# A linear-attention step on one core: the state product regrouped by pairs of sequences, and VectorE's step reordered

## The reference

```python
xn  = layernorm(x)
q   = softmax(exp(beta) * (xn @ Wq.T + bq), over the 8 features of a head)
k   = softmax(exp(beta) * (xn @ Wk.T + bk), over the 8 features of a head)
v   = xn @ Wv.T + bv
kv  = cumsum over tokens of k^T v        # per head an 8x8 state
kn  = cumsum over tokens of k
att = (q @ kv) / sum(q * kn)
ffn = fp8_round(xn) @ weight_fp8.T + bias
out = x + att @ Wo.T + bo + ffn
```

## Time and profile before

| | before |
|---|---|
| time, median of 3 runs | 1250.92 us (1249.5 to 1252.77) |
| span of the profiled execution, first to last instruction | 1248.2 us |
| PE busy | 1174.9 us, 94% of the span |
| DVE busy | 977.9 us, 78% |
| ACT busy | 744.9 us, 60% |
| POOL busy | 321.6 us, 26% |
| chain that ended last | PE 92%, issue 3%, DVE 2%, DMA, ACT and POOL 1% each |
| granted PE clock, mean over the span | 0.982 of full speed |

### The profile page before, as it was taken

One profiled execution on the slowest core, in us unless ns is written; L12 is line 12 of the kernel. 1 busy time (PEld: TensorE's weight loads), 2 busy tenths in 40 slices (PEclk: granted clock), 3 DMA queues, 4 the chain that ended last, 5 costly groups with the idle time before them and its releaser, 6 DMA issues.

```text
span 1248.2 us, 60447 instructions
## 1 busy us (share of the span) xinstructions
PE 1174.9 (94%) x26082; PEld 679.2 (54%) x26082; DVE 977.9 (78%) x1968; ACT 744.9 (60%) x1177; POOL 321.6 (26%) x590
## 2 busy tenths in 40 slices
PE   1459999999999999999999999999999999999996
PEld 1235555555555555555555555555555555555553
DVE  4567887888788788878878887788788778878873
ACT  0456656665666666566666656666665666566652
POOL 3122222322222232222223232222323232222310
PEclk9689999999999999999999999999999999999999
DMA  9022334334334433433333343343343433333331
GB/s 234 21 59 70 81 90 89 78 80 91 82 82 87 89 80 79 90 86 80 85 89 82 77 90 89 78 84 91 81 79 91 84 83 81 91 82 81 72 73 46
DMA packets 156483, 104.64 MB, mean 84 GB/s; under 512 B 111968, under 2 KB 128480, under 8 KB 156256
## 3 DMA queue, kind: packets, MB, share of 16 engines
q1 hardware_dynamic: 155536, 99.76, 35.7%
q10 hardware_dynamic: 720, 1.31, 0.4%
HBM read 40.20 MB, written 16.78 MB: 46 GB/s over the span
## 4 chain that ended last, share of the span: by engine, by line
PE 92%; issue 3%; DVE 2%; DMA 1%; ACT 1%; POOL 1%; SPq 0%; POOLq 0%; DVEq 0%; ACTq 0%
PE s_ps L900 10%; PE a_ps L917 7%; PE a_ps L1018 6%; PE a_ps L999 6%; PE k_ps L873 5%; PE vo_ps L975 5%; PE vo_ps L873 5%; PE k_ps L877 5%; PE k_ps L875 5%; PE vo_ps L884 4%; PE vo_ps L888 4%; PE vo_ps L886 4%; PE vo_ps L877 4%; PE vo_ps L875 4%; PE q_ps L877 4%; PE q_ps L873 4%
## 5 line engine op out<-in xcount | busy, mean ns | idle before, releaser
L521 ACT ACTIVATE q_heads<-qT,cst 128x512 f32<-128x512 f32 x256 | 163.9, 711 | 88.2 <-DVE qT L769 88.2
L407 POOL TENSOR_TENSOR y_sum<-y,y_magic 128x512 f32<-128x512 f32 x64 | 81.4, 1272 | 433.0 <-DVE y_magic L629 433.0
L506 ACT ACTIVATE w_own<-kT,cst 128x512 f32<-128x512 f32 x128 | 85.5, 715 | 166.7 <-DVE kT L711 166.7
L530 ACT ACTIVATE st_seqs<-st_run,cst 128x576 f32<-128x576 f32 x252 | 181.5, 797 | 0.5 <-DVE st_run L665 0.5
L671 DVE TENSOR_TENSOR att<-s_ps,cst 128x512 f32<-128x512 f32 x256 | 163.8, 682 | 0.4 <-PE s_ps L900 0.4
L400 POOL TENSOR_TENSOR x_split<-xn,x_split 128x512 f16<-128x512 f32 x64 | 74.1, 1158 | 291.6 <-ACT x_split L462 284.3
L900 PE MATMUL s_ps<-q_heads,w_own 64*64 64x128 f32 x4096 | 141.3, 275 | 0.6 <-DVE att L671 0.6
L900 PEld LDWEIGHTS s_ps<-q_heads,w_own 64*64 64x64 f32 x4096 | 110.4, 132 | 54.3 <-issue 54.2
L462 ACT ACTIVATE x_split<-xn 128x512 f16<-128x512 f32 x64 | 40.3, 630 | 126.7 <-DVE xn L618 126.7
L873 PE MATMUL k_ps<-w_hi,xT 128*128 128x512 f16 x256 | 98.9, 386 | 17.0 <-DMA xT<-x_split 12.3
L727 DVE TENSOR_TENSOR vp<-vo_ps,vp 128x512 f32<-128x512 f32 x64 | 44.3, 692 | 86.3 <-PE vo_ps L877 86.3
(11 more groups left out here) (136 smaller groups left out, 2287.8 us busy)
## 6 DMA issues: line engine op xcount, KB each, us to landing
v_groups<-vp SPq DMA_DIRECT2D x512, 36.0 KB, 3.1
x_in<-L_attn_x SPq DMA_DIRECT2D x64, 256.0 KB
x_res<-L_attn_x SPq DMA_DIRECT2D x64, 256.0 KB
out<-o_sb SPq DMA_DIRECT2D x64, 256.0 KB
w_own<-L_attn_Wk SPq DMA_DIRECT2D x1, 1024.0 KB, 13.0
w_own<-L_attn_Wq SPq DMA_DIRECT2D x1, 1024.0 KB, 15.0
w_own<-L_attn_Wv SPq DMA_DIRECT2D x1, 1024.0 KB, 16.5
att<-L_ffn_weight_fp SPq DMA_DIRECT2D x1, 1024.0 KB, 18.1
```

The lines of the kernel that those rows point to most:

```text
L506: last = sc.activation(k_pairs[:, i.parity, :, c, :], kT[:, :, :], ACT.Copy, scale=pair_mask[:, c:c + 1])
L521: last = sc.activation(q_heads[:, i.parity, :, j, :], qT[:, i.parity, :, :], ACT.Copy, scale=head_mask[:, j:j + 1])
L530: last = sc.activation(st_seqs[:, i.parity, :, :, b, :].rearrange("p g j w -> p (g j) w"), st_run[:, :, :, :].rearrange("p g j w -> p (g j ...
```

## The change

Four things change, all inside a round.

1. **State product.** It becomes 32 matmuls instead of 64: for each of 16 head groups and each *pair* of sequences, 64 tokens (two sequences on 64 partitions) are multiplied with 72 columns, 36 for either sequence of the pair. So that the two sequences don't mix, the columns of one are zero on the partitions of the other. The result has the head group's place in a quarter of the partitions, and the sequence in its columns. It is written in one piece behind the second half of the scores.
2. **POOL** makes these columns: a new `pair_values` multiplies `vp` of 576 columns with a mask, once for each sequence of the pair, at the head of its round. `v_pairs` lies in the place of the weights `w_own[0]`, which are no longer needed by then.
3. **ACT** builds `st_seqs` with 16 copies of 32 partitions x 144 elements instead of 4 of 128 x 576, and without a mask; the blocks between stay zero from the start (POOL clears the second buffer once).
4. **DVE's round** is written in another order: statistics before the key shift, rounding constant and variances before `al`, both state masks together before the second score half, output before `qT`.

PE's *intra* product is also issued as two halves with a wait each, in the same place. The core of the diff:

```diff
-            def state(t, n):
-                if n == 0:
-                    pe.wait_ge(ke_ready, (t + 1).n)
-                    pe.wait_ge(vp_ready, (t + 1).n)
-                    if t.after(1):
-                        pe.wait_ge(an_ready, t.n)
-                    pe.sem_inc(pe_waited, 1)
-                for g in range(n * G // 2, (n + 1) * G // 2):
-                    col = DM * n + J * VW * (g % (G // 2))
-                    for b in range(SEQS):
-                        rows = slice(TOK * b, TOK * (b + 1))
-                        last = mm(a_ps[rows, col:col + J * VW], k_e[rows, t.parity, TOK * g:TOK * (g + 1)],
-                                  vp[rows, t.parity, v_head(g):v_head(g) + J, :], start=True, stop=True)
-                last.then_inc(state_done, 1)
+            def state(t):
+                pe.wait_ge(ke_ready, (t + 1).n)
+                pe.wait_ge(vpairs_ready, (t + 1).n)
+                if t.after(1):
+                    pe.wait_ge(an_ready, t.n)
+                pe.sem_inc(pe_waited, 1)
+                for c4 in range(G // J):
+                    for u in range(J):
+                        g = J * c4 + u
+                        for n in range(SEQS // SP):
+                            rows = slice(SP * TOK * n, SP * TOK * (n + 1))
+                            col = DM * n + SP * J * VW * c4
+                            last = mm(a_ps[TOK * u:TOK * (u + 1), col:col + SP * J * VW],
+                                      k_e[rows, t.parity, TOK * g:TOK * (g + 1)],
+                                      v_pairs[rows, :, v_head(g):v_head(g) + J, :]
+                                      .rearrange("p c j w -> p c (j w)"), start=True, stop=True)
+                last.then_inc(state_done, 1)
...
+            def pair_values(t):
+                pool.wait_ge(vp_ready, (t + 1).n)
+                if t.after(1):
+                    pool.wait_ge(state_done, t.n)
+                for c in range(SP):
+                    last = gp.tensor_tensor(v_pairs[:, c].rearrange("p h w -> p (h w)"),
+                                            vp[:, t.parity].rearrange("p h w -> p (h w)"),
+                                            pair_mask[:, c:c + 1].to_broadcast([P, HEADS * VW]), ALU.mult)
+                last.then_inc(vpairs_ready, 1)
...
                     for b in range(SEQS):
-                        last = sc.activation(st_seqs[:, i.parity, :, :, b, :].rearrange("p g j w -> p (g j) w"),
-                                             st_run[:, :, :, :].rearrange("p g j w -> p (g j) w"),
-                                             ACT.Copy, scale=seq_mask[:, b:b + 1])
+                        for u in range(J):
+                            last = sc.activation(st_seqs[TOK * b:TOK * (b + 1), i.parity, u::J, :, b, :],
+                                                 st_run[TOK * u:TOK * (u + 1), b // SP, :, b % SP, :, :],
+                                                 ACT.Copy)
```

More of the change, by code:

```diff
@@ L526, in body @@
                     act.wait_ge(strun_ready, (t + 1).n)
+                    if not t.after(1):
+                        act.wait_ge(st_cleared, 1)
                     if t.after(1):
@@ new lines, in turn_attention @@
+            def turn_attention(t):
+                pe.wait_ge(an_ready, (t + 1).n)
+                if t.after(1):
+                    pe.wait_ge(al_ready, t.n)
+                else:
+                    pe.wait_ge(bvl_ready, 1)
+                for b in range(SEQS):
+                    last = transpose(t_ps[:, :].rearrange("p (j b s) -> p b j s", b=SEQS, s=TOK)[:, b],
+                                     a_n[:, b, :, :].rearrange("p g d -> p (g d)"), ident)
+                last.then_inc(aT_done, 1)
@@ new lines, in quantised @@
+            def quantised(t, low_part):
+                pe.wait_ge(xq_turned, (t + 1).n * 16)
+                pe.wait_ge(oseed_ready, (t + 1).n)
+                for c in range(KC):
+                    last = mm(vo_ps[:, :], xq[:, t.slot, c, :], w_hi[:, MF, c, :], start=False,
+                              stop=False, skip_group_check=True)
+                    if low_part:
+                        last = mm(vo_ps[:, :], xq[:, t.slot, c, :], w_lo[:, MF, c, :], start=False,
+                                  stop=False, skip_group_check=True)
+                last.then_inc(f_done, 1)
@@ new lines, in output_product, with inter @@
+            def output_product(t):
+                pe.wait_ge(ah_ready, (t + 1).n)
+                pe.wait_ge(al_ready, (t + 1).n)
+                project_out(rest=True).then_inc(o_done, 1)
+            def inter(t, more):
+                pe.wait_ge(qT_ready, (t + 1).n)
+                if more:
+                    pe.wait_ge(masked_ready, (t + 1).n)
+                else:
+                    pe.wait_ge(an_ready, t.n)
+                if t.after(1):
+                    pe.wait_ge(stseqs_ready, t.n)
+                for n in range(2):
+                    for gp in range(GP):
+                        for u in range(J):
+                            g = G // 2 * n + GP * u + gp
+                            mm(a_rows[TOK * u:TOK * (u + 1), n, gp, :], qT[:, t.parity, g, :],
+                               st_seqs[:, t.parity, g].rearrange("p j b w -> p (j b w)"),
+                               start=(gp == 0), stop=False, skip_group_check=True)
@@ L932, in body @@
                     scores(t, 0)
-                    if i.exists():
-                        state(t, 0)
-                t = i - 2
-                if t.exists():
-                    pe.wait_ge(an_ready, (t + 1).n)
-                    if t.after(1):
-                        pe.wait_ge(al_ready, t.n)
-                    else:
-                        pe.wait_ge(bvl_ready, 1)
-                    for b in range(SEQS):
-                        last = transpose(t_ps[:, :].rearrange("p (j b s) -> p b j s", b=SEQS, s=TOK)[:, b],
-                                         a_n[:, b, :, :].rearrange("p g d -> p (g d)"), ident)
-                    last.then_inc(aT_done, 1)
+                if d.exists():
+                    turn_attention(d)
@@ L1024, in transpose_weights @@
+                    inter(t, i.exists())
+                if i.exists():
+                    values(i, fold)
+                if t.exists():
+                    intra(t, 0)
+                    intra(t, 1)
             def transpose_weights(m):
```

202 lines of the change are left out of this document (94 added, 108 removed).

## The result

The changed kernel takes 1316.52 us (median of 4 runs, 1315.74 to 1316.91) against 1250.6 us: ratio 1.0522, 95% interval 1.0507 to 1.0537. It is 5.2% slower, where 1.1% faster was forecast. Its profiled span is 1314.9 us, 66.7 longer than before.

What follows compares the result with a forecast made beforehand. PE bounded the old kernel; afterwards DVE's rounds of 18.32 and 17.51 us, mean 17.92 against 18.14, save 14 us over 62 rounds: 1248.2 - 14 + 2.7 = 1237 us, range 1212 to 1265.

Steps and rivals of the forecast that it cites:

- Then 16 cost 16 x 0.23 = 3.7 us: ACT's spread: 16 copies of 144 elements, neighbours overlapping by 0.09 us, cost 3.7 us against 2.88 before.
- the second rival: ACT's spread: copies don't overlap since partitions change; S = 5.1, ring 18.3 us, 1261 us, up to 1266; chance 0.28.
- The ring's sum: Loop through DVE and ACT from `qT` back to `qT`: 16.9 us a round, below PE's and DVE's sums.
- 13.2 + S: Ring length in us: 13.2 for all else, S for ACT's spread, taken as 3.7.
- the prediction's 3.79: DVE's stretch `al` to `y_exp` in the ring: 3.79 us in the mean, 3.94 less 0.3 every second round.
- VectorE's chain: DVE's work from round start to `o_sb`: 13.67 us with variances, 12.86 without; rounds 17.79 and 16.98 before the hold.
- The hold: DVE's `xn` waits until POOL's second product ends: 0 to 0.53 us a round, upper end taken.
- PE's sum: PE's round: 18.00 - 1.38 for two state halves + 0.67 for the new group = 17.29 us, if nothing waits.
- The two rivals on tiles: PE's state product: only four tiles at once, 1246 us, chance 0.09; tiles sharing weights' partitions in turn, 1295 us, chance 0.03.
- what would show it: Trace signs listed beforehand: state group's length, `xn` to `xq_rows`, spread and `ah`, PE's waits, gap before the reciprocal.
- the two marks of 0.45 and 1.0: DVE's `xn` start to `xq_rows`: growth from 0.45 to about 1.0 us would show `xn` held.

Runs made afterwards that it cites:

- the cuts of the old spread: Kernel before, its 4 spread copies cut into 16 of 144 elements: masked on 128 partitions (1250.57 us, ratio 0.9999), unmasked on 128, unmasked on 32.
- the spread shared: Changed kernel with 8 of the spread's 16 copies moved from ACT to VectorE: 1263.62 us, ratio 1.0102 to the kernel before.

## Why the prediction was wrong, step by step

**The step that failed: "Then 16 cost 16 x 0.23 = 3.7 us".** They cost 5.43. The duration was right (318 ns expected, 328 measured); the overlap with the neighbour was not there, because each copy reads or writes other partitions than the one before. That was the second rival, and its own reason, with a chance of 0.28; the cuts of the old spread show it (0.21 us without a change, 0.32 to 0.33 at one), and the changed kernel's 0.34 fits, with the element pattern left open as said. Its condition (over 0.30 us a copy; measured 0.34) was met.

**The ring's sum was right, and not by luck.** 13.2 + S gives 18.6 at S = 5.43; the rounds without variances took 18.50. In the trace of such a round, from one `qT` to the next, everything but the spread is 13.05 us; the other 0.15 is the gap before the reciprocal, which the prediction's 3.79 had in it by half and these rounds don't have. Moving the spread out of the ring and changing nothing else shows that it binds.

**A second step failed, in the rival as in the forecast: what a round with variances costs.** The rival's ring at 5.43 gives 18.6 us for every round, some 1281 us, not 1316; its own price, 1261 to 1266, was lower still, because it took S = 5.1. The prediction put the variances at 0.51, in VectorE's chain alone, and averaged the ring over both kinds of round. It did not ask which arrival releases VectorE in them. There it is `y`, and behind `y` stand the rounding constant, the variances and `al`: 1.16 us more from `y_magic` to `al`, of which 0.95 is POOL's `y_sum` on top of `guess`. Moving the variances, their own 0.5 us and the hold, gave back 35 us.

**The hold was seen and put at the wrong place.** I priced it at 0.53 for `xn`, "all of what is left of POOL's instruction". For `xn` it is what is left less 0.26: 0.24 here, 0.63 of 0.89 with the spread shared. With the products left out the time didn't move. The hold that counted, that of `guess` by `y_sum`, is by a POOL instruction that was there before; the new order put VectorE's work under it. So is that of `y_exp` by `x_split`, 0.54 us. Without variances it fills time in which VectorE would wait for `ah` in any case; with them it can add to the round, but no run takes it away alone. The prediction looked only at the instructions that the change added.

**PE's sum**: the group takes 0.81 us, not the 0.67 of 0.63 to 0.69. PE's round is 17.43 and not 17.29, 9 us in the whole, and it is seen only where PE bounds again. The two rivals on tiles fall: 1.12 to 1.24 with four at work, 2.2 for tiles that share the weights' partitions. The Trainium skill's rule for the latter ("TensorE: Matmul & The Clock Gate", section "Part 3: Packing small matmuls — row/col tiling"), that a weight load overlaps running matmuls only when its row group differs, doesn't describe this group: it took 0.81 us.

**VectorE's chain** from its start to the end of `o_sb` was right: 12.86 + 0.24 against 13.07 us read in the run with the spread behind `ah` and the variances moved (a round without variances). It bounds nothing while the ring is longer.

**Of what would show it**: inter no longer waiting for the state mask was wrong, it waits 1.26 us and PE 0.6 us more at the values, where the wait for `o_sb` came as forecast; the gap before the reciprocal stayed, in the rounds with variances, and its cause was not tested; `ah` was not ready before VectorE asked (0.19 us in the rounds without variances); `xn` to `xq_rows` grew to 0.71 us, between the two marks of 0.45 and 1.0; PE never waits for the products, as forecast.

## What to carry to other kernels

When an instruction moves, ask of both kinds of round which arrival releases it, and lay the other engine's timeline over its new place: work that cost nothing may now run under someone's hold. A ring is shortened by changing places on an engine that waits elsewhere in the round; one such move was worth 68 us here (1316.5 to 1248.9) without removing anything. And an engine's price per instruction holds only for the pattern in which it was measured; many small copies that hop between partitions are another pattern.

## What was not expected of the hardware

- ACT's neighbouring copies overlap by 0.10 us when they keep to the same partitions (0.21 us apart at 0.316 us each) and not where the partitions change (0.32 to 0.33 us apart at the three changes on 32 partitions, 0.34 at 0.328 us each in the changed kernel).
- A VectorE instruction of two columns that touches only SBUF is held by POOL as a wide one is: 1.06 us in the mean instead of 0.17 (`guess` under `y_sum`), 1.13 (`var_e` under `x_split`). A reduction or a transposition was not held: `k_sum` takes 0.67 us with `y_round` beside it, and `kT` 0.65 with it and without.
- A held instruction of 512 columns ends 0.28 us after POOL's, whenever it began, and one of two columns 0.03. So a hold costs what was left of POOL's instruction plus that, less the time that the instruction takes alone: for `xn` (0.54 alone) 0.26 less than what was left, for `y_exp` and `xq_rows` (0.42 and 0.41) 0.13 or 0.14 less.
